# A selective scan re-laid: channels as lanes and states as ticks, with B's row spread by the matrix engine, C's by DMA, and the sum over states on GpSimd

## The reference, cut to what matters

```python
dbc = x @ x_proj_w                      # x: silu of a short convolution, 128 channels
dt, Bm, Cm = ...                        # 4, 16 and 16 columns of dbc
delta = softplus(dt @ dt_proj_w + dt_proj_b)
A = -exp(A_log)                         # 128 channels x 16 states
def step(h, inp):                       # h: 128 x 16
    d_t, u_t, b_t, c_t = inp
    h = exp(d_t[..., None] * A) * h + (d_t * u_t)[..., None] * b_t[:, None, :]
    y = einsum('bdn,bn->bd', h, c_t)    # sum over the 16 states
    return (h, y)
y = scan(step) + x * D                  # then * silu(z), @ out_proj_w
```

## Time and profile before

| | |
|---|---|
| median of three runs | 8327.68 us |
| profiled execution | 8337.88 us, span 8336.1 us |
| mean granted TensorE clock | 0.943 |
| busy: TensorE / VectorE / ScalarE / GpSimd | 7452.2 / 6635.4 / 5857.4 / 3402.1 us |
| DMA | 1555.68 MB, mean 187 GB/s |
| convolutions | about 0 to 900 us |
| ticks that scan | 2048, until about 7906 us |
| last ticks, attention alone | to the end |

### The profile page before, as it was taken

One profiled execution on the slowest core, in us unless ns is written; L12 is line 12 of the kernel. 1 busy time (PEld: TensorE's weight loads), 2 busy tenths in 40 slices (PEclk: granted clock), 3 DMA queues, 4 the chain that ended last, 5 costly groups with the idle time before them and its releaser, 6 DMA issues. The chain is left out here.

```text
span 8336.1 us, 144239 instructions
## 1 busy us (share of the span) xinstructions
PE 7452.2 (89%) x44358; PEld 2739.2 (33%) x44358; DVE 6635.4 (80%) x10726; ACT 5857.4 (70%) x10454; POOL 3402.1 (41%) x4133
## 2 busy tenths in 40 slices
PE   9962489999999999999989999999999999999999
PEld 2311133333333333333333333333333333333333
DVE  2238888888989888898878888888889898888831
ACT  1124477777878777787777777777778787777765
POOL 0015544444444444444444444444444444444400
PEclk9985589999999999999999999999999999999999
DMA  9838878778787877887777888788887878777710
GB/s 152 134 95 216 213 198 205 203 197 206 197 205 202 200 198 199 201 207 197 202 186 200 200 203 206 194 204 203 204 204 194 206 199 200 203 197 204 186 36 11
DMA packets 855509, 1555.68 MB, mean 187 GB/s; under 512 B 400008, under 2 KB 418256, under 8 KB 854736
## 3 DMA queue, kind: packets, MB, share of 16 engines
q1 hardware_dynamic: 852688, 1545.93, 75.8%
q10 hardware_dynamic: 2048, 0.53, 0.0%
HBM read 1335.08 MB, written 193.72 MB: 183 GB/s over the span
## 5 line engine op out<-in xcount | busy, mean ns | idle before, releaser
L1267 POOL TENSOR_TENSOR hst<-hst,cbc 128x512 f32<-128x512 f32 x2048 | 2619.2, 1279 | 3642.1 <-DVE bank L1144 3620.1
L1155 DVE TENSOR_TENSOR_SCAN hst<-dA,carry,bank 128x512 f32<-128x512 f32 x1792 | 2294.2, 1280 | 131.1 <-DVE bank L1144 42.6
L844 PE MATMUL bank<-kx,qr 96*128 96x512 f32 x4096 | 2043.5, 500 | 276.0 <-DVE mxp L1098 135.4
L1015 ACT ACTIVATE pr<-bank 128x512 f32<-128x512 f32 x4096 | 2220.7, 601 | 40.2 <-PE bank L908 38.8
L919 PE MATMUL bank<-pr,vt 128*32 128x512 f32 x16384 | 2248.6, 622 | 0.0
L960 ACT ACTIVATE gains<-bank 128x512 f32<-128x512 f32 x2048 | 1219.5, 595 | 1052.6 <-PE bank L844 665.4
L1021 ACT ACTIVATE dA<-lanes,small 128x512 f32<-128x512 f32 x2048 | 1497.9, 731 | 608.5 <-DMA lanes<-spread_d 560.0
L1144 DVE TENSOR_TENSOR bank<-lanes,bbc 128x512 f32<-128x512 f32 x2048 | 1516.6, 741 | 328.0 <-DMA lanes<-spread_d 197.8
L1098 DVE CUSTOM_DVE_ANT_0 gains<-bank,gains 128x512 f32<-128x512 f32 x2048 | 1368.6, 668 | 267.6 <-PE bank L844 261.1
L908 PE MATMUL bank<-qr,kr 98*128 98x512 f32 x4096 | 1424.6, 417 | 169.6 <-ACT pr L1015 163.6
L844 PEld LDWEIGHTS bank<-kx,qr 96*128 96x128 f32 x4096 | 780.9, 191 | 1828.6 <-issue 1078.9
(11 more groups left out here) (108 smaller groups left out, 4999.9 us busy)
## 6 DMA issues: line engine op xcount, KB each, us to landing
lanes<-spread_d SPq DMA_DIRECT2D x2048, 512.0 KB, 6.5
seqt<-seq_d SPq DMA_DIRECT2D x256, 128.0 KB, 4.8
spread_d<-dsp SPq DMA_DIRECT2D x128, 256.0 KB, 2.0
spread_d<-usp SPq DMA_DIRECT2D x128, 256.0 KB, 2.0
bbc<-bc_d SPq DMA_DIRECT2D x128, 256.0 KB, 3.5
cbc<-bc_d SPq DMA_DIRECT2D x128, 256.0 KB, 4.3
kx<-kx_d SPq DMA_DIRECT2D x192, 128.0 KB, 4.9
qr<-parts_d SPq DMA_DIRECT2D x192, 128.0 KB, 4.9
```

The costliest lines, as they stand in the source:

```text
L844: mm = nc.tensor.matmul(bank[:].rearrange("p (c n) -> p c n", n=HALF), qr[0:SPLIT, ring_slot((a, q)), nt * P:(nt + 1) * P].bitcast(F32R), ...
L1015: nc.scalar.activation(pr[:, T % PRING, h, :], bank_of(("S", T, h))[:], ACT.Exp).then_inc(S["p_full"], 1)
L1155: nc.vector.tensor_tensor_scan(hst[:, slot_of(T), :], dA[:, T % 2, :], DBU[:], carry[:, g:g + 1] if sl % CHUNKS else 0.0, ALU.mult, ALU.ad ...
L1267: nc.gpsimd.tensor_tensor(h, h, cbc[:, (T - 1) // GROUPS % 2, :], ALU.mult).then_inc(S["hc_in"], 1)
```

## The change

- A tick is now one state n, and its 128 lanes are the 128 channels. `GROUPS` is 16 as before, so the number of ticks stays. `delta` and `du` stay in SBUF; `lanes`, `dsp`, `usp`, `bbc` and `carry` go, with their DMAs. dA is made from `delta`, with the column n of `amat` as scale.
- B's row n has to be on all 128 lanes. TensorE does this in every tick with one fp32r matmul of 128 rows x 128 columns x 512 (`spread_b`): the weights are a 0/1 column repeated 128 times, the moving operand `bhl` holds B split in a high part and a rest. It goes into one of two banks `BB`, is written ahead of the tick's dif, and waits for the scan two ticks before its own. VectorE multiplies the bank by `du` in place.
- With two banks for BB instead of one for DBU, RING goes from 5 to 4.
- C's row n is repeated on 128 lanes by one DMA of 256 KB in each tick, into a ring of five slots that GpSimd alone reads.
- GpSimd multiplies into `ysum` or `hct`, out of place, and adds `hct` to `ysum` in three ticks of four. Its wait for `dbu_in` is gone. TensorE adds the four sums of a chunk with four identity matmuls (fp32, 128 x 128 x 512).
- y moves from r = 2 to 3, `ysb` from 3 to 4, its product with z from 4 to 5.
- BC is one fp32 matmul of 32 columns x 512. ScalarE copies it out twice and VectorE subtracts for the rest (the new `BC` in VectorE's small uses).

```diff
-RING = 5
+RING = 4
-        name = {2: "y", 7: "out", 12: "xv", 14: "en"}.get(r)
+        name = {3: "y", 7: "out", 12: "xv", 14: "en"}.get(r)
-    RB, (DBU, ACC, DEN) = banks[0:RING], banks[RING:]
+    RB, BB, (ACC, DEN) = banks[0:RING], banks[RING:RING + 2], banks[RING + 2:]
...
-                            issued(sp.dma_start(spread_d[c % 2, :, 0, :], dsp[:]), "st_sp")
...
-                            issued(sp.dma_start(spread_d[c % 2, :, 1, :], usp[:]), "st_sp")
...
-                            wait(sp, "st_sp", X // GROUPS, 32)
-                            wait(sp, "da_in", X - SLOTS)
-                            wait(sp, "dbu_in", X - SLOTS)
...
-                            issued(sp.dma_start(lanes[:, X % SLOTS].rearrange("p w l -> p (w l)"),
-                                                near.partition_broadcast(D_STATE)), f"lanes{X % SLOTS}")
+                            wait(sp, "st_c", X // GROUPS, 16)
+                            wait(sp, "hc_in", X - SLOTS)
+                            issued(sp.dma_start(cbc[:, c_slot(X), :],
+                                                c_d[X // GROUPS % 2, X % GROUPS].partition_broadcast(P)),
+                                   f"c{c_slot(X)}")
...
-                            for j in range(BLOCKS):
-                                mm = nc.tensor.matmul(bank[BLOCK * j:BLOCK * (j + 1), 0:P], wbc[:],
-                                                      u[:, c % 2, P * j:P * (j + 1)], start=True, stop=True,
-                                                      tile_position=(0, BLOCK * j))
+                            mm = nc.tensor.matmul(bank[0:2 * D_STATE, :], wbc[:], u[:, c % 2, :],
+                                                  start=True, stop=True)
...
-                            wait(pe, "hc_in", GROUPS * (c + 1) - 1)
-                            for gl in range(GPB):
-                                for j in range(BLOCKS):
-                                    mm = nc.tensor.matmul(
...
+                            wait(pe, "hadd", GROUPS * (c + 1) - 1)
+                            for g in range(YGROUPS):
+                                mm = nc.tensor.matmul(bank[:], ident, ysum[:, y_slot(GROUPS * c + GROUP * g), :],
+                                                      start=g == 0, stop=g == YGROUPS - 1)
...
+                    def spread_b(X):
+
+                        c, n = X // GROUPS, X % GROUPS
+                        taken(pe, ("BC", c))
+                        wait(pe, "scan", X - 2)
+                        nc.tensor.matmul(BB[X % 2][:], sel[:, n:n + 1].bitcast(F32R).broadcast_to([P, P]),
+                                         bhl[:, c % 2, :].bitcast(F32R), start=True, stop=True).then_inc(S["bb_in"], 1)
+
                     for T in range(first, last):
+                        if sched.spreads(T + 1):
+                            spread_b(T + 1)
...
-                            nc.scalar.activation(dA[:, (T + 1) % 2, :], lanes[:, (T + 1) % SLOTS, 0, :], ACT.Exp,
-                                                 scale=amat[:, g:g + 1]).then_inc(S["da_in"], 1)
+                            nc.scalar.activation(dA[:, (T + 1) % 2, :], delta[:, X % 2, :], ACT.Exp,
+                                                 scale=amat[:, n:n + 1]).then_inc(S["da_in"], 1)
...
-                            nc.vector.tensor_tensor(DBU[:], lanes[:, T % SLOTS, 1, :], bbc[:, sl % 2, :],
-                                                    ALU.mult).then_inc(
-                                S["dbu_in"], 1)
+                            wait(dve, "bb_in", T)
+                            wait(dve, "du_in", sl)
+                            nc.vector.tensor_tensor(BB[T % 2][:], BB[T % 2][:], du[:, sl % 2, :],
+                                                    ALU.mult).then_inc(S["dbu_in"], 1)
...
-                            if due("dbu_in", T):
-                                pool.wait_ge(S["dbu_in"], due("dbu_in", T))
-                            h = hst[:, slot_of(T - 1), :]
-                            nc.gpsimd.tensor_tensor(h, h, cbc[:, (T - 1) // GROUPS % 2, :],
+                            if X % GROUP == 0:
+                                into = ysum[:, y_slot(X), :]
+                                full_wait(pool, ("y", X // GROUPS - (2 if X % GROUPS == 0 else 1)))
+                            else:
+                                into = hct[:, X % 2, :]
+                                wait(pool, "hadd", X - 2)
+                            nc.gpsimd.tensor_tensor(into, hst[:, X % GROUPS, :], cbc[:, c_slot(X), :],
                                                     ALU.mult).then_inc(S["hc_in"], 1)
+                        if sched.scans(T - 2) and T % GROUP != 2:
+                            X = T - 2
+                            wait(pool, "hc_in", X)
+                            wait(pool, "hadd", X - 1)
+                            nc.gpsimd.tensor_tensor(ysum[:, y_slot(X), :], ysum[:, y_slot(X), :], hct[:, X % 2, :],
+                                                    ALU.add).then_inc(S["hadd"], 1)
```

More of the change, by code:

```diff
@@ L89, in shape_constants @@
     c[:, C_ID:C_ID + P] = np.eye(P)
-    for lane in range(P):
-        for g in range(GPB):
-            row = DL * g + lane % DL
-            c[lane, C_SUM + BLOCK * g + row] = 1
-    return c
-def group_of(T):
-    k = T % GROUPS
-    return k % BLOCKS * GPB + k // BLOCKS
-def slot_of(T):
-    k = T % GROUPS
-    return k if k >= HALVES or T // GROUPS % 2 == 0 else k + GROUPS
+    for n in range(D_STATE):
+        c[n, C_SEL + n] = c[BLOCK + n, C_SEL + n] = 1
+    return c
 class Span:
@@ L148, in scans @@
         return self.image(T // TICKS)
-    def carries(self, T):
-        return self.scans(T) and T >= 0 and T % TICKS < TICKS - GROUPS
     def spreads(self, T):
@@ L235 @@
 SIGNAL_OF = {"PV": "pv", "SUM": "den"}
-DVE_USES = ("max", "turn", "mix", "res", "en", "y")
-RING = 5
+DVE_USES = ("max", "turn", "mix", "res", "en", "y", "BC")
+RING = 4
 def build(nc, x, w1, b1, w2, b2, w_in, cw, cb, w_dt_t, w_dt, dt_b, w_bc, a_log, skip, w_out,
@@ L464, in pipeline @@
         em1 = sb("em1", [P, CHUNK])
[L465 to L467 removed]
+        delta = sb("delta", [P, 2, CHUNK])
+        du = sb("du", [P, 2, CHUNK])
         dA = sb("dA", [P, 2, CHUNK])
[L469 to L470 removed]
+        hst = sb("hst", [P, GROUPS, CHUNK])
+        hct = sb("hct", [P, 2, CHUNK])
+        ysum = sb("ysum", [P, YRING, CHUNK])
         ysb = sb("ysb", [P, CHUNK])
@@ L952, in small_use @@
                         kind, c = e[0], e[1]
+                        if kind == "BC":
+                            wait(act, "st_c", c - 1, 16)
+                            full_wait(act, e)
+                            rows = slice(0, 2 * D_STATE)
+                            nc.scalar.copy(bcs[:], bank_of(e)[rows]).then_inc(S["c_out"], 1)
+                            wait(act, "bb_in", GROUPS * (c - 1) - 1)
+                            nc.scalar.copy(bhl[rows, c % 2, :].bitcast(F32R), bank_of(e)[rows]).then_inc(S["b_hi"], 1)
+                            return
                         if kind in DVE_USES:
@@ L975, in small_use @@
                             wait(act, "delta_in", c - 1)
-                        elif kind == "BC":
-                            wait(act, "st_bc", c - 1, 16 * BLOCKS)
                         elif kind == "out":
@@ L1132, in _ @@
                         c = sl - 1
-                        if sched.chunk(c) and r == 3:
+                        if sched.chunk(c) and r == 4:
                             full_wait(dve, ("y", c))
@@ new lines, in _ @@
+                            wait(pool, f"c{c_slot(X)}", X, 16)
+                            if due("scan", X):
+                                pool.wait_ge(S["scan"], due("scan", X))
+                            if X % GROUP == 0:
[4 more added lines that the diff above has]
+                                wait(pool, "hadd", X - 2)
@@ L1269, in _ @@
                         c = sl - 1
-                        if sched.chunk(c) and r == 4:
+                        if sched.chunk(c) and r == 5:
                             taken(pool, ("y", c))
```

140 lines of the change are left out of this document (53 added, 87 removed).

## The result

The changed kernel takes 9112.01 us (median of four runs, 9103.81 to 9122.72) against 8324.83 us for the kernel before (8303.63 to 8336.23): ratio 1.095, 95% interval 1.093 to 1.098. It is 787 us slower. The forecast had the direction (+427 over the median) and was short in size; 9112 lies above the range of 8280 to 9080. The profiled span is 9102.0 us at the same mean granted clock as before, 0.943.

What follows compares the result with a forecast made beforehand. VectorE and TensorE were taken to set the pace in turn: 57.8 + 0.1 + 3.6 (collisions) = 61.5 us a chunk, +3.7 over 118 chunks, 437 us, giving 8765 us; range 8280 to 9080.

Steps and rivals of the forecast that it cites:

- What bounds the kernel: Whole chunk of 16 ticks, 57.8 us: VectorE and TensorE set the pace in turn; the DMA engines, busy 0.80, do not.
- TensorE's leg: Scan of r = 12 to the next ysb, usually 24.3 us: +4.1 us from the change, less 0.3 for lane waits.
- VectorE's work without collisions: From ysb to the scan of r = 12: the change takes 3.7 us a chunk off VectorE, collisions aside.
- The collisions' term: VectorE's elementwise instructions delayed by GpSimd's product at r = 5, 6, 7, 8, 10: 3.6 us a chunk, range 0 to 8.
- VectorE's leg: Stretch from ysb (r = 3) to the scan of r = 12, about 32 us, in which VectorE never waits.
- the upper bound: At r = 7: if L1195 collides, GpSimd's addition slips in before L1197, 1.8 us; 1.0 was taken.
- What is left without collisions: Whole chunk with collisions left out: 0.4 us longer, net +0.1 after 0.3 given back for lane waits.
- rival 3: TensorE's heavy ticks, with less run-ahead and four banks, make VectorE late: 3 us more a chunk, 9120 us; chance 0.12.
- Rival 1: Collisions cost nothing because VectorE's late ticks are made up behind TensorE: 8340 us; chance 0.13.
- rival 2: The lanes' DMA waits caused TensorE's long leg, so removing them makes the kernel faster: 8150 us; chance 0.17.
- the lanes' waits: Waits for `lanes`, 4.4 us a chunk on ScalarE and 1.5 on VectorE, mostly hidden: 0.3 us given back.
- The signs to look for: Changed profile: about 260 scans per 1000 us, elementwise means of 1.3 us or more, DMA below half, both legs filled.

Runs made afterwards that it cites:

- a_behind: Changed kernel, complete, with GpSimd's product waiting until VectorE's elementwise instruction of the same tick is done (r = 3, 5, 6, 7, 8, 10); 8518.13 us, ratio 1.024.
- a_noadd_under: Changed kernel without GpSimd's additions (y incomplete) and with GpSimd's product put behind VectorE's product of the tick; 8483.45 us, ratio 1.021.
- b_free: Kernel before with only GpSimd's wait for VectorE's product taken out; 9247.20 us, ratio 1.113.
- b_ring4: Kernel before with four banks in the ring instead of five and one bank unused; 8525.66 us, ratio 1.025.
- b_ring4_mm: Kernel before with four ring banks and one more matmul a tick into the eighth bank, which nobody reads; 8552.36 us, ratio 1.027.
- a_fix_bcheap: Changed kernel with GpSimd's product behind VectorE's elementwise instruction, ysb x z at r = 6, and B's spread over 64 of 512 columns; 8451.99 us, ratio 1.015.
- a_fix_xv: Changed kernel with GpSimd's product behind VectorE's elementwise instruction, ysb x z at r = 6, xv and en one tick earlier; 8501.60 us, ratio 1.022.

## Why the prediction was wrong in size

- **What bounds the kernel**: right. Two legs that take turns; the DMA at 0.80 was no bound. Its traffic fell from 1556 to 880 MB and no kernel shows a gain from it that can be told.
- **TensorE's leg**: right as a sum, 30.0 forecast and 29.6 measured, but by luck in part. B's spread was priced at 2.2 us a chunk; the runs that take seven eighths of it away give 0.4 and 0.5, the run that adds a matmul a tick 0.2. The taps' collisions were put at nothing here, with 5 us to spare; the taps took 1.26 us instead of 0.75, and a_behind's leg, with the third one free and a higher clock, is 28.5.
- **VectorE's work without collisions**: right. The forecast's steps take 3.7 us off 31.4 us of busy time: 27.7. In a_noadd_under, where in this leg u alone still collides (1.51 instead of 0.69), VectorE is busy for 28.55, and 27.7 without that. (One label is off: the product of 1.47 us in the earlier trace rows is that of r = 5, in the same leg.)
- **The collisions' term, first failed step.** The mechanism is right and shown by removing it (a_behind) and by making it (b_free). The size was wrong: "Sum 3.6" for VectorE's leg, and it is 6.6. By the means of the lines: u +0.75, z +0.79, L1192 +0.68 and low +0.89 over its least are 3.1 where the sum has 2.6; L1175 +0.78 and L1177 +0.96 are 1.7 where it has 1.0; and four instructions that stand in every second chunk, L1214 +0.95, L1094 +0.99, L1209 +1.08 and L1093 +0.44, add half of 3.46, 1.7, where it has nothing, since I listed instructions by what every chunk has. Together 6.6, and the busy time says the same: 34.3 measured less 27.7. The missing 3.0 us times 118 are 354 us, all of the 347 between 8765 and 9112. At r = 7 no row of the kernel before could decide, and the rule of the Trainium skill (SBUF — State Buffer, Who interferes with whom), that VectorE's two-port modes, which a tensor_scalar can enter, contend with GpSimd too, was the better guide: L1175 at 1.20 instead of 0.42 agrees with it, and the addition slipped in just as the upper bound had it.
- **What is left without collisions, second failed step.** "So without collisions the chunk becomes 0.4 us longer", and 0.1 after the lanes: a_behind, where most of them are gone, keeps 205 us, 1.7 a chunk. The sum took VectorE's leg to be as long as VectorE is busy, but in a_noadd_under it is 30.7 us long with 28.55 busy: it is no longer VectorE alone that sets its pace. I named the four banks in rival 3 and priced them with a pattern of heavy ticks instead of in the sum; b_ring4 prices them at 213 us, 1.8 a chunk. Rival 3's total of 9120 is close to what was measured, but of its 3 us only these 1.8 are shown, and B's wait for the scan was not tried by itself.
- **Rival 1** (collisions hidden behind TensorE) and **rival 2** (lanes were the cause) are both refuted, the first by a_behind, the second by the measured ratio of every complete kernel with the new layout. What the lanes' waits gave back by themselves (0.3 in the sum) no run shows.
- **The signs to look for**: held, save the number of scans (247 instead of 260), VectorE filling its leg throughout (34.04 of 35.71) and L1212, now L1192, which stood at 0.42 before, not at 0.69, and now at 1.10, not at 1.3.

The two failed steps are not parts of one sum. Seen from the changed kernel, whose VectorE is busy for 34.3 of 35.0 us of its leg, the collisions account for the whole shortfall. Seen from the kernel with most of them removed, 594 us are the collisions (with what the clock gave back) and 205 something else; these two add up to the loss by construction and prove nothing about each other. That the 205 are mostly the bank, and some 60 of them the spread, is an argument from kernels near by (b_ring4, b_ring4_mm, a_fix_bcheap); a_behind's remaining collisions and the new subtraction at r = 10 are in them too. The changed layout with five ring banks and two for B cannot be built with eight banks, so it was not tried. No version of the new layout beats the kernel before: the best complete one, a_fix_xv, is at 1.022.

## What to carry to other kernels

- A wait that shows only as idle time of one engine can be what keeps it out of another's way: without GpSimd's 3620 us of waiting the kernel takes 937 us more. Before such a wait goes, list every VectorE instruction with its inputs in SBUF that can stand in the new window, those of every second chunk too, and price each at the other engine's remaining time.
- Put GpSimd's big instructions where VectorE reads PSUM or scans, tick by tick. Six waits gave back three quarters of the loss.
- Price a PSUM bank like an instruction. Two banks for an operand meant one fewer for run-ahead, and in the kernel before that one is worth 2.5%.
